# Flamingo-style two-layer block on one core: five maxima over partitions taken by TensorE and VectorE instead of GpSimd, and the order of every engine written out anew for each group

## The chip, the cores and the metric

The kernel runs on one core of a Trainium2 chip. The metric is the device time of one execution in microseconds, the median of several runs. The core has five engines that each work through their own instructions strictly in order: TensorE (PE in the profile; its weight loads are shown as PEld), VectorE (DVE), ScalarE (ACT), GpSimd (POOL) and SyncE (SP), which here only starts DMAs. They wait for one another by semaphores.

## The reference

Input x is 2 x 2048 tokens of 512 numbers, ctx is 2 x 128 tokens of 512. Four blocks follow one another; each adds tanh(gate) times its output to x, and each starts with a layer norm.

```python
x = x + tanh(g_xattn[0]) * attention(layernorm(x), ctx, Wq, Wkv, Wout)   # 8 heads, rotary q and k, 128 keys
x = x + tanh(g_ffn[0]) * ffn0(layernorm(x))      # ternary weights w_fc, w_proj with row scales,
                                                 # plus gate * low rank (u, fast_b, v); relu, square; 512-2048-512
x = x + tanh(g_xattn[1]) * (layernorm(x) @ W1.T + mean_over_ctx(ctx) @ W2.T + b)
x = x + tanh(g_ffn[1]) * ffn1(layernorm(x))      # int8-like activations, ternary weights w1, w2
                                                 # scaled by their mean |w|; exact gelu; 512-2048-512
```

Ternary weights are round(w / scale) clipped to -1, 0, 1; the scale of ffn0 is the mean |w| of a row, that of ffn1 the mean over the matrix. The weights arrive as float32 and are quantised inside the kernel.

## The kernel before, in words

**Tiling.** The 4096 tokens are cut into 16 groups of 256 (GROUPS; two tiles t of 128 tokens each). Every group g runs through the same steps: ln1, q projection (`q`), rotary, scores (`s`, four units n of one tile and half the heads), softmax (`max`, `exp`, `sum`, `norm`), attention times v (`pv`), output projection (`wo`), ln2, low-rank rows (`low`), first ffn (`up` in 8 units of two 128-row blocks, `down` in 8 pieces: 4 for each tile), ln3, the mix (`wx`), ln4, the second ffn (`w1` in 8 pieces, gelu, `w2`), and the store. Float32 activations enter matmuls as a pair of fp16 parts (hi and lo): ACT writes the hi part, DVE or POOL the rest, and a transposing DMA (from SP) turns them.

**Setting up.** Ahead of and among group 0 stand the steps that prepare the weights (`prepare` on each engine). Three of the weights (Wq, Wout, the mix's W1) and k, v and the low-rank v are scaled by their largest |value| before they are split into fp16 pairs. Each such maximum is taken in two steps: DVE reduces along the free dimension into one column (`abs_max`, into wmax or kvmax), and POOL's `partition_all_reduce` (L701, in `largest`) takes the largest of the 128 partitions and writes it to all of them (wmaxa, kvmaxa). There are five calls: Wq; k and v together; Wout and v of the low rank together; a bound on the hidden values (bmax to bmaxa, from which the scale rho of the hidden layer comes); and W1 of the mix. `weight_scale`, `kv_scale` and `hidden_scale` on DVE wait for them. The eight pieces of w_fc and w_proj are compared with thresholds on DVE (`signs`, L1052 and L1058), turned by PE (`tern`, L1481) and copied by ACT (`evac`, L807). The first `up` of group 0 needs all of w_fc, the row scales (`row_scale`, L1532 on PE and L1240 on DVE) and the low-rank rows of group 0.

**What sets the order.** No scheduler decides it. A table gives every step of every engine a place, a number; `moments` sorts the numbers of an engine, and `run` issues the steps whose number has come (`due` for the groups' steps, `here` for preparation). In the kernel before, table AT has one number per step, and group g uses it with g x 65536 added; groups 0, 1, 2, 14 and 15 have numbers of their own in table OWN. So groups 3 to 13 follow one another in one fixed pattern. On PE that pattern is, from one low-rank product to the next (g is the group in the first ffn, g+1 is in its attention, g-1 and g-2 are in the second ffn):

```text
low.g up0.g w2(t1).g-2 q0.g+1 q1.g+1 up1.g up2.g up3.g up4.g s0.g+1 wx1.g-1 up5.g s1 s2 up6.g s3 up7.g
w1(0..2).g-1 down0.g w1(3..5).g-1 down1.g down2.g down3.g w1(6).g-1 pv0 down4.g pv1 w1(7).g-1 wo0 wo1 w2(t0).g-1
down5.g down6.g down7.g wx0.g
```

**Places the prediction speaks of.** `low_rows` (L1609) writes the low-rank product to PSUM; ACT copies it as bf16 (`low_first`, L910); DVE makes the three-part bf16 tile tlow (`low_parts`, L1335 to L1340); the last matmul of each block of `up` (L1633) reads tlow, the first time in unit 0. `down` (L1645) waits for POOL's `hid_low` (L674), the lo part of the hidden values, two units for each piece. `out_proj` (`wo`, L1596) waits for the DVE lo part of the attention output (L1269). `scores` (L1570) waits for the four DMAs of `pair_heads` (q_in), which wait for the chain of rotary (DVE L1282 to L1285, POOL L669, ACT L875, DVE L1269) after `q_proj` (L1551).

## Time and profile before

| what | us |
|---|---|
| median of 3 runs | 1346.24 |
| lowest and highest of them | 1342.70, 1351.59 |
| span of the profiled execution, first to last instruction | 1340.0 |
| PE, DVE, ACT, POOL busy in it | 1135.0, 974.3, 788.0, 597.8 |

The profiled execution's own device time is not listed apart from the runs; its span lies 6.2 us under their median, and that much is taken as what lies around a span. Rows of the trace give start and length in microseconds of an instruction (or of a run of like ones, with xcount), then its engine, line, operation and tiles; a bracket at the end says how long the engine stood idle before it and whose result ended the wait. "issue" there means that the profile shows no wait: the engine was fetching or setting something up. Durations of pipelined matmuls overlap, so PE's work is better read from start to start.

### The profile page before, as it was taken

To read this page: it belongs to the slowest core of one execution; us is meant where nothing else is said; L and a number is where in the kernel's file an instruction comes from. 1 tells how busy PE (TensorE), PEld (TensorE's weight loads), DVE (VectorE), ACT (ScalarE), POOL (GpSimd) and SP (SyncE) were. 2 spreads that over 40 slices of the span, in tenths; PEclk is the share of its full clock that TensorE was granted. 3 is DMA by queue.
4 is the path that set the end of the run, shared out by engine and by line. 5 is a ranking of instruction groups with operands and counts; after the bars stand their busy time and mean duration, and the time that the engine had idled before them with its cause. 6 is when DMAs were issued, how large, how long until landed. Compare 5 with 4: busy or idle time off the path is not lost.

```text
span 1340.0 us, 19939 instructions
## 1 busy us (share of the span) xinstructions
PE 1135.0 (85%) x7092; PEld 695.2 (52%) x7380; DVE 974.3 (73%) x2017; ACT 788.0 (59%) x1509; POOL 597.8 (45%) x569
## 2 busy tenths in 40 slices
PE   4353777989898999999999999999999988899975
PEld 3332545546374646555564747464656556475621
DVE  3895587887758676877778686868687776877574
ACT  2455773839465574838384656657483838475523
POOL 1221254645534535455463555454545435363430
PEclk9666898999999999999999999999999999999997
DMA  6957744353423444443635343444444343524132
GB/s 220 298 179 214 238 135 97 78 111 71 91 67 84 98 87 100 87 97 81 130 79 100 70 87 77 96 98 87 99 87 87 87 99 74 114 55 86 24 67 51
DMA packets 302241, 140.28 MB, mean 105 GB/s; under 512 B 258096, under 2 KB 276016, under 8 KB 300464
## 3 DMA queue, kind: packets, MB, share of 16 engines
q1 hardware_dynamic: 299840, 136.62, 44.4%
q10 hardware_dynamic: 2304, 2.40, 0.6%
q8 instruction: 57, 0.93, 0.3%
q14 instruction: 40, 0.33, 0.1%
HBM read 57.97 MB, written 9.18 MB: 50 GB/s over the span
## 4 chain that ended last, share of the span: by engine, by line
DVE 27%; PE 27%; ACT 21%; POOL 12%; issue 9%; DMA 3%; SPq 1%; DVEq 0%; POOLq 0%; ACTq 0%
ACT e L882 6%; PE ps L1693 5%; PE ps L1645 5%; PE ps L1629 4%; DVE st L1256 4%; PE ps L1551 3%; PE ps L1596 3%; ACT rl L920 3%; POOL rs L649 2%; DVE amax L986 2%; ACT hid L925 2%; ACT sq L931 2%; POOL hid L674 2%; POOL e L679 2%; POOL r L692 2%
## 5 line engine op out<-in xcount | busy, mean ns | idle before, releaser
L1629 PE MATMUL ps<-xT,fcT 128*128 128x256 f16 x2048 | 261.1, 275 | 1.9 <-DVE scbc L1240 1.0
L1645 PE MATMUL ps<-pjT,hid 128*128 128x512 fp8e4 x1024 | 239.4, 385 | 24.1 <-POOL hid L674 22.0
L649 POOL TENSOR_TENSOR rs<-ve,nhalf 128x1 f32<-128x1 f32 x160 | 100.6, 629 | 289.1 <-DVE ve L1261 220.0
L1629 PEld LDWEIGHTS ps<-xT,fcT 128*128 128x128 fp8e4 x2048 | 201.0, 99 | 33.7 <-ACT rl L920 4.3
L674 POOL TENSOR_TENSOR hid<-sq,hid 128x512 f16<-128x512 f32 x128 | 163.0, 1280 | 101.8 <-ACT sq L931 101.8
L1645 PEld LDWEIGHTS ps<-pjT,hid 128*128 128x128 f16 x1024 | 98.5, 99 | 100.8 <-issue 4.9
L1693 PE MATMUL ps<-w2T,hT 128*128 128x512 fp8e4 x512 | 130.1, 413 | 12.5 <-DMA hT<-q 12.5
L1681 PE MATMUL ps<-w1T,q4T 128*128 128x512 fp8e4 x512 | 127.9, 390 | 15.0 <-DMA q4T<-x16b 6.5
L920 ACT ACTIVATE rl<-ps,rsf 128x256 f32<-128x256 f32 x256 | 106.6, 470 | 38.4 <-PE ps L1633 38.2
L679 POOL TENSOR_TENSOR e<-e,einv 128x512 f32<-128x512 f32 x64 | 73.1, 1142 | 125.7 <-DVE einv L1303 116.1
L882 ACT ACTIVATE e<-ps,nmb,sig 128x128 f32<-128x128 f32 x256 | 113.0, 455 | 13.3 <-DVE nmb L1299 13.0
L1269 DVE TENSOR_TENSOR qT<-e,qT 128x512 f16<-128x512 f32 x96 | 79.6, 830 | 50.9 <-ACT qT L893 28.6
L1551 PE MATMUL ps<-pt,wq 128*128 128x256 f16 x768 | 88.9, 276 | 13.2 <-DMA pt<-x16a 11.7
L1661 PE MATMUL ps<-wx,xT 128*128 128x512 f16 x384 | 92.2, 392 | 7.1 <-DMA xT<-x16b 7.1
L1402 DVE SCALAR_TENSOR_TENSOR h<-ps,dqs,b1bc 128x512 f32<-128x512 f32 x128 | 91.6, 740 | 8.8 <-PE ps L1681 8.3
L1633 PE MATMUL ps<-tlow,lowA 128*128 128x256 bf16 x256 | 71.2, 278 | 30.1 <-DVE tlow L1340 30.1
L1596 PE MATMUL ps<-wo,qS 128*128 128x512 f16 x384 | 86.3, 381 | 9.1 <-DVE qS L1269 9.1
L952 ACT ACTIVATE q<-h 128x2048 f16<-128x2048 f32 x32 | 61.1, 1908 | 52.4 <-DVE h L1413 52.4
L1551 PEld LDWEIGHTS ps<-pt,wq 128*128 128x128 f16 x768 | 75.9, 99 | 26.5 <-issue 14.7
L1693 PEld LDWEIGHTS ps<-w2T,hT 128*128 128x128 f16 x512 | 53.2, 105 | 64.6 <-issue 18.7
L669 POOL TENSOR_TENSOR e<-e 128x512 f32<-128x512 f32 x32 | 43.9, 1371 | 92.5 <-DVE e L1285 84.5
L875 ACT ACTIVATE qT<-e 128x512 f16<-128x512 f32 x32 | 20.1, 627 | 109.1 <-POOL e L669 109.1
(202 smaller groups left out, 2112.1 us busy)
## 6 DMA issues: line engine op xcount, KB each, us to landing
qS<-qT SPq DMA_DIRECT2D x128, 64.0 KB, 2.1
xb<-in_x SPq DMA_DIRECT2D x16, 512.0 KB, 4.8
out<-r SPq DMA_DIRECT2D x32, 256.0 KB, 2.6
xa<-in_x SPq DMA_DIRECT2D x15, 512.0 KB, 4.0
rope<-in_rope SPq DMA_DIRECT2D x16, 384.0 KB, 3.6
h<-in_w1T SPq DMA_DIRECT2D x6, 1024.0 KB, 6.5
h<-in_w2T SPq DMA_DIRECT2D x6, 1024.0 KB, 7.3
h<-in_wkvT SPq DMA_DIRECT2D x2, 1024.0 KB, 15.3
```

What stands on the lines that cost most here:

```text
L649: pool.tensor_tensor(rs[:, n, t:t + 1], ve[:, n, t:t + 1], nhalf[:, :], ALU.pow).then_inc(done, 1)
L674: pool.tensor_tensor(flat[:, 1, :], sq[:, m % 2, :], flat[:, 0, :], ALU.subtract).then_inc(hid_lo, 1)
L679: pool.tensor_tensor(view, view, einv[:, n, :].unsqueeze(2).broadcast_to([P, 4, S]), ALU.mult)\
L882: last = act.activation(e[:, n, a * S:(a + 1) * S], att_bank(2 + n)[:, a * S:(a + 1) * S], ACT.Exp, bias=nmb[:, n, a:a + 1], scale=sig[:, ...
L920: act.activation(rl[:, m % 2, a * G:(a + 1) * G], ps[:, FFN0 + m % 2, a * G:(a + 1) * G], ACT.Relu, scale=rsf[:, 2 * m + a:2 * m + a + 1]) ...
L1551: mm = pe.matmul(att_bank(hg)[:, a * G:(a + 1) * G], wq[:, ws, k, c:c + P], xT1[:, xs, k, :], start=(n == 0 and k == 0), stop=(n == 2 and ...
L1596: mm = pe.matmul(att_bank(8 + t), ao[:, xs, k, t * P:(t + 1) * P], wo[:, ws, k, :], start=(n == 0 and k == 0), stop=(n == 2 and k == KC - 1))
L1629: pe.matmul(dst, fcT[:, k, f * P:(f + 1) * P], xT2[:, xs, k, :], start=(xs == 0 and k == 0), stop=False)
L1645: mm = pe.matmul(ps[:, FFN0 + t, :], hid[:, xs, c, t * P:(t + 1) * P], pjT[:, c, :], start=(c == 0 and xs == 0), stop=(c == FC - 1 and xs ...
L1661: mm = pe.matmul(back_bank(t), xT3[:, xs, k, t * P:(t + 1) * P], wx[:, ws, k, :], start=(n == 0 and k == 0), stop=(n == 2 and k == KC - 1))
L1681: mm = pe.matmul(back_bank(2 + u), q4T[:, k, t * P:(t + 1) * P], w1T[:, k, n * 512:(n + 1) * 512], start=(k == 0), stop=(k == KC - 1))
L1693: mm = pe.matmul(back_bank(10 + t), hT[:, t, c, :], w2T[:, c, :], start=(c == 0), stop=(c == FC - 1))
```

## The change

Two things are changed.

1. `partition_all_reduce` and POOL's five calls are gone. For each of the five maxima DVE now multiplies the identity by the column (`spread_diag`: a 128x128 diagonal, one or two of them in the new tile dg), PE multiplies a matrix of ones by it (`spread`: every partition then holds the whole column along its free dimension, in PSUM), and DVE takes the maximum along that row (`largest`). The matmul is float32. Five pieces of PSUM are used for it (SPREAD), in banks of the attention and of the second ffn; the first scores wait for the third maximum, the mean's matmul for the fifth.
2. The tables AT and OWN, with numbers in nanoseconds that repeat from group 3 to 13, are replaced by one table ORDER that gives each step of each group a rank on its engine. Every group has its own row of it. PREP holds ranks in the same numbering.

```diff
+        SPREAD = ((ATT0 + 2, 1), (ATT0 + 2, 2), (ATT0 + 2, 2), (BACK0 + 2, 1), (BACK0 + 2, 1))
...
-        AT = dict(
-            PE=dict(up=(195289, 200771, 211516, 211832, 213196, 215372, 223295, 232242),
...
+        ORDER = dict(
+            PE=dict(
+                up=((35, 36, 37, 39, 40, 41, 44, 46), (64, 65, 66, 70, 74, 75, 79, 80),
...
-            def largest(ready, count, done, dst, src):
-
-                pool.wait_ge(ready, count)
-                pool.partition_all_reduce(dst, src, P, RMAXOP).then_inc(done, 1)
...
+            def spread_diag(n, ready, count, cols):
+
+                dve.wait_ge(ready, count)
+                if n == 0:
+                    dve.wait_ge(c_const, 5)
+                else:
+                    dve.wait_ge(c_mxps, n)
+                for j, col in enumerate(cols):
+                    last = dve.tensor_scalar(dg[:, j, :], ident[:, :], col, None, ALU.mult)
+                last.then_inc(c_mxd, 1)
+
+            def largest(n, dst):
+
+                dve.wait_ge(c_mxps, n + 1)
+                dve.tensor_reduce(dst, spread_to(n).rearrange("p (c n) -> p c n", n=P), axis=AX.X, op=ALU.max)\
+                    .then_inc(c_mx, 1)
+                dve.wait_ge(c_mx, n + 1)
...
-                dve.wait_ge(c_wmaxa, n + 1)
+                largest(n, wmaxa[:, a:b])
...
-                dve.wait_ge(c_bndmax, 1)
+                largest(3, bmaxa[:, :])
...
+            def spread(n):
+
+                if n > 0:
+                    pe.wait_ge(c_mx, n)
+                pe.wait_ge(c_mxd, n + 1)
+                pe.matmul(spread_to(n), ones[:, :], dg[:, 0:SPREAD[n][1], :].rearrange("p c n -> p (c n)"),
+                          start=True, stop=True).then_inc(c_mxps, 1)
...
-                    pe.wait_ge(c_low, 3)
+                    pe.wait_ge(c_mx, 5)
...
                 if first(g) and n == 0:
+                    pe.wait_ge(c_mx, 3)
                     pe.wait_ge(c_kblk, 1)
```

How POOL's instructions stand at the start of the program. Before, from the first rsqrt of ln1 of group 0 (L649) to the last softmax `norm` of group 0 (L679); L701 is the all-reduce, and each row that says only ISA is an instruction of the kind that sets the engine up for the operation behind it:

```order
L649 TENSOR_TENSOR rs<-ve,nhalf 128x1
L701 ISA
L701 ISA wmaxa<-wmax 128x1
L649 ISA
L649 TENSOR_TENSOR rs<-ve,nhalf 128x1
...
L679 TENSOR_TENSOR e<-e,einv 128x512
L701 ISA
L701 ISA bmaxa<-bmax 128x1
L679 ISA
L679 TENSOR_TENSOR e<-e,einv 128x512
L701 ISA
L701 ISA wmaxa<-wmax 128x1
```

Now, the same place (L719 rsqrt, L723 the lo part of x, L786 the context sums, L766 rotary of k, L791 a clearing of lowF, L739 rotary of q, L749 `norm`):

```order
L719 TENSOR_TENSOR rs<-ve,nhalf 128x1 x2
L723 TENSOR_TENSOR x16a<-xa,x16a 128x512
L786 TENSOR_TENSOR r<-ones,csum 128x128 x8
L723 TENSOR_TENSOR x16a<-xa,x16a 128x512
L766 TENSOR_TENSOR x3n<-x3n,rl 128x512 x2
L791 MEMSET x3n 128x2048
L739 TENSOR_TENSOR e<-e 128x512 x2
L719 TENSOR_TENSOR rs<-ve,nhalf 128x1 x2
L723 TENSOR_TENSOR x16a<-xa,x16a 128x512 x2
L749 TENSOR_TENSOR e<-e,einv 128x512 x4
```

No set-up instruction is left between them, the four norms follow one another, and ln1 of group 1 (rsqrt and lo part) has moved ahead of them.

PE's instructions in the steady part, around the low-rank product of group 8 (L1609 before). L1629 and L1633 are a block of `up`, L1691 and L1693 are `w2`, L1551 is `q`, L1661 `wx`, L1645 `down`:

```order
L1645 MATMUL ps<-pjT,hid 128x512 x8
L1661 MATMUL ps<-wx,xT 128x512 x12
L1609 MATMUL ps<-xT,vrep 128x256 x12
L1629 MATMUL ps<-xT,fcT 128x256 x8
L1633 MATMUL ps<-tlow,lowA 128x256
L1629 MATMUL ps<-xT,fcT 128x256 x8
L1633 MATMUL ps<-tlow,lowA 128x256
L1691 LDWEIGHTS hT
L1693 MATMUL ps<-w2T,hT 128x512 x16
L1551 MATMUL ps<-pt,wq 128x256 x48
```

Now, the same place (L1698 the low-rank product, L1718 and L1722 `up`, L1780 and L1782 `w2`, L1750 `wx`, L1639 `q`, L1659 scores):

```order
L1782 MATMUL ps<-w2T,hT 128x512 x16
L1750 MATMUL ps<-wx,xT 128x512 x12
L1639 MATMUL ps<-pt,wq 128x256 x24
L1698 MATMUL ps<-xT,vrep 128x256 x12
L1639 MATMUL ps<-pt,wq 128x256 x24
L1780 LDWEIGHTS hT
L1782 MATMUL ps<-w2T,hT 128x512 x16
L1718 MATMUL ps<-xT,fcT 128x256 x8
L1722 MATMUL ps<-tlow,lowA 128x256
...
L1659 MATMUL ps<-kv,qS 128x256 x6
```

Before, `up` stood directly behind the low-rank product; now half of `q` and a `w2` stand between. The next group is written otherwise again: behind its low-rank product comes only the `w2`, and then the first scores. In groups 3 to 12 something stands there each time (`w2`, `wx`, or both, at times with half of `q`), in group 13 nothing.

PE again, later in the same group: from the last piece of `w1` (L1681) that stood before `down1`, over `pv` (L1584), to `wo` (L1596). Before:

```order
L1645 MATMUL ps<-pjT,hid 128x512 x8
L1642 LDWEIGHTS hid
L1645 MATMUL ps<-pjT,hid 128x512 x8
L1679 LDWEIGHTS q4T
L1681 MATMUL ps<-w1T,q4T 128x512 x4
L1584 MATMUL ps<-pt,kv 64x256 x12
L1642 LDWEIGHTS hid
L1645 MATMUL ps<-pjT,hid 128x512 x8
L1584 MATMUL ps<-pt,kv 64x256 x12
L1679 LDWEIGHTS q4T
L1681 MATMUL ps<-w1T,q4T 128x512 x4
L1596 MATMUL ps<-wo,qS 128x512 x24
```

Now (L1734 `down`, L1770 `w1`, L1673 `pv`, L1685 `wo`):

```order
L1734 MATMUL ps<-pjT,hid 128x512 x8
L1673 MATMUL ps<-pt,kv 64x256 x12
L1731 LDWEIGHTS hid
L1734 MATMUL ps<-pjT,hid 128x512 x8
L1673 MATMUL ps<-pt,kv 64x256 x12
L1731 LDWEIGHTS hid
L1734 MATMUL ps<-pjT,hid 128x512 x8
L1768 LDWEIGHTS q4T
L1770 MATMUL ps<-w1T,q4T 128x512 x4
L1685 MATMUL ps<-wo,qS 128x512 x24
```

Both `pv` stand earlier among the `down` pieces, `down4` (first piece of the second tile) has moved ahead of `down1`, and `down3`, which needs the last hidden values, now stands behind the second `pv`.

## Rows read from the trace of the kernel before

**Rows 1.** The page's head and its first part: busy time and share of each engine

```profile
span 1340.0 us, 19939 instructions
PE 1135.0 (85%) x7092; PEld 695.2 (52%) x7380; DVE 974.3 (73%) x2017; ACT 788.0 (59%) x1509; POOL 597.8 (45%) x569
```

**Rows 2.** Two stretches: length; busy PE, PEld, DVE, ACT, POOL; PE clock; DMA share; GB/s

```profile
0.00:153.40 153.40, 67.59 (x377) 46.29 (x378) 99.87 (x205) 75.84 (x128) 31.73 (x43) 0.73 0.72 226
...
480.00:1056.00 576.00, 536.68 (x3413) 329.16 (x3553) 431.04 (x922) 356.08 (x705) 288.07 (x272) 0.97 0.44 89
```

**Rows 3.** PE's waits from 480 to 1056 us: total, times, longest

```profile
PE ps L1633 <- DVE tlow L1340: 18.6, 8, 2.3
PE ps L1645 <- POOL hid L674: 15.6, 8, 1.9
PE ps L1596 <- DVE qS L1269: 4.0, 8, 0.5
```

**Rows 4.** PE in order of time, one group of the fixed pattern

```profile
655.28 1.47 PE L1609 MATMUL ps<-xT,vrep 128*128 128x256 f16 x12
...
659.94 0.39 PE L1633 MATMUL ps<-tlow,lowA 128*128 128x256 bf16 x1 [2.31 <-DVE tlow L1340]
660.12 1.92 PE L1629 MATMUL ps<-xT,fcT 128*128 128x256 f16 x8
...
662.04 4.29 PE L1693 MATMUL ps<-w2T,hT 128*128 128x512 fp8e4 x16
666.17 5.40 PE L1551 MATMUL ps<-pt,wq 128*128 128x256 f16 x48
671.41 1.04 PE L1629 MATMUL ps<-xT,fcT 128*128 128x256 f16 x8
...
679.51 0.82 PE L1570 MATMUL ps<-kv,qS 128*128 128x256 f16 x6
...
703.37 2.67 PE L1645 MATMUL ps<-pjT,hid 128*128 128x512 fp8e4 x8 [1.95 <-POOL hid L674]
...
717.87 3.62 PE L1693 MATMUL ps<-w2T,hT 128*128 128x512 fp8e4 x16
```

**Rows 5.** POOL in order of time, 15 to 120 us

```profile
18.33 0.38 POOL L701 PARTITION_ALL_REDUCE wmaxa<-wmax  x1 [8.16 <-issue]
26.04 0.59 POOL L649 TENSOR_TENSOR rs<-ve,nhalf 128x1 f32<-128x1 f32 x1 [7.33 <-issue]
...
88.52 2.43 POOL L701 PARTITION_ALL_REDUCE bmaxa<-bmax  x1 [5.89 <-issue]
99.87 2.04 POOL L679 TENSOR_TENSOR e<-e,einv 128x512 f32<-128x512 f32 x1 [8.91 <-DVE einv L1303]
108.83 0.79 POOL L701 PARTITION_ALL_REDUCE wmaxa<-wmax  x1 [6.92 <-issue]
119.20 1.03 POOL L679 TENSOR_TENSOR e<-e,einv 128x512 f32<-128x512 f32 x1 [9.58 <-issue]
```

**Rows 6.** DVE in order of time, 10 to 147 us

```profile
10.53 2.29 DVE L986 TENSOR_REDUCE wmax<-hid 128x1 f32<-128x2048 f32 x1 [1.00 <-DMA hid<-in_wqT]
...
26.66 1.38 DVE L1265 TENSOR_SCALAR xa<-xa,mv,rs 128x512 f32<-128x512 f32 x1 [7.57 <-POOL rs L649]
...
103.98 0.17 DVE L1303 RECIPROCAL einv<-esum 128x4 f32<-128x4 f32 x1
...
120.98 0.69 DVE L1269 TENSOR_TENSOR qT<-e,qT 128x512 f16<-128x512 f32 x1 [9.61 <-ACT qT L893]
...
130.03 0.87 DVE L1234 TENSOR_SCALAR r<-ident,scd 128x128 f32<-128x128 f32 x4
...
146.67 0.17 DVE L1245 TENSOR_REDUCE wmean<-ps 128x2 f32<-128x8 f32 x1 [3.24 <-PE ps L1537]
```

**Rows 7.** PE in order of time, the two float32 matmuls by the matrix of ones

```profile
131.04 2.05 PE L1532 MATMUL ps<-r,ones 128*128 128x512 f32 x2 [3.08 <-DVE r L1234]
...
146.04 0.60 PE L1537 MATMUL ps<-wsum,ones 128*128 128x8 f32 x2 [6.20 <-ACT hT L857]
```

More of the change, by code:

```diff
@@ new lines, in build @@
+        PREP = dict(
+            PE=dict(k=(1, 2), v=(3, 4), low=(7,), mix=(11,), tern=(5, 18, 19, 20, 21, 23, 25, 26), low_t=(22,),
+                    row_scale=(28,), mean=(32,), spread=(0, 6, 8, 12, 16)),
+            DVE=dict(const=(0,), ctx_sum=(7,), rot_k=(9, 11), wq_max=(1,), wq_scale=(5,), k_max=(12,), wq_lo=(8,),
+                     v_max=(15,), kv_scale=(18,), k_lo=(20,), v_lo=(21, 22), signs=(14, 17, 25, 50, 54, 57, 60, 64),
+                     thr=(13, 16, 24, 32, 34, 42, 44, 63), wo_max=(10,), v_top=(19,), wo_scale=(23,), k_other=(37,),
+                     wo_lo=(31,), mix_row=(59,), low_rank=(33,), v_parts=(62,), wx_max=(38,), hidden=(40,),
+                     wx_scale=(48,), wx_lo=(67,), row_scale=(69,), mean=(76,), k_now=(36,), diag=(66,),
+                     round=(77, 79, 84, 87, 93, 95, 100, 114), clip=(80, 81, 88, 91, 96, 108, 109, 120)),
+            ACT=dict(wq=(1,), k_hi=(6,), v_hi=(7, 8), tanh=(5,), wo=(10,), kv_save=(17,),
+                     evac=(22, 25, 29, 33, 36, 38, 41, 44), rows=(3, 4, 9, 12, 14, 15, 16, 18), low=(37,), wx=(32,),
+                     sums=(30, 35, 39, 42, 45, 46, 47, 49), lift=(51, 52, 56, 58, 62, 75, 76, 82)),
+            POOL=dict(rot_k=(5, 6), csb=(3,), low_zero=(7,), above=(0, 0, 0, 0, 0, 0, 0, 0)),
+            SP=dict(ctx=(1,), wk=(2,), wq=(0,), wv=(3,),
+                    piece=(5, 7, 11, 15, 16, 17, 19, 21, 26, 28, 31, 34, 36, 30, 33, 39, 40, 41, 45, 46, 49, 50, 52, 57),
+                    wo=(4,), wc=(6,), wx=(8,), b1=(18,), k_pair=(20,)))
@@ L449, in moments @@
+        placed = {}
+        for eng, tables in ORDER.items():
+            for name, rows in tables.items():
+                for g, places in enumerate(rows):
+                    for k, p in enumerate(places):
+                        placed.setdefault((eng, name, p), []).append((k, g))
         def moments(eng):
@@ L716, in prepare @@
                     rotate_k(hg)
-                for _ in here("POOL", "wq_max", p):
-                    largest(c_wmax, 1, c_wmaxa, wmaxa[:, 0:1], wmax[:, 0:1])
-                for _ in here("POOL", "kv_max", p):
-                    largest(c_kvmax, 2, c_kvmaxa, kvmaxa[:, :], kvmax[:, :])
                 for _ in here("POOL", "csb", p):
@@ L727, in prepare @@
                     last.then_inc(c_csb, 1)
-                for _ in here("POOL", "wo_max", p):
-                    largest(c_wmax, 3, c_wmaxa, wmaxa[:, 1:3], wmax[:, 1:3])
                 for _ in here("POOL", "low_zero", p):
@@ L735, in prepare @@
                         signs_above(q)
-                for _ in here("POOL", "bound", p):
-                    largest(c_bnd, 4, c_bndmax, bmaxa[:, :], bmax[:, :])
-                for _ in here("POOL", "wx_max", p):
-                    largest(c_wmax, 4, c_wmaxa, wmaxa[:, 3:4], wmax[:, 3:4])
             def run():
@@ L1171, in prepare @@
                     abs_max(kvmax[:, 1:2], ps[:, 0:2, :].rearrange("p b n -> p (b n)"), c_kvmax)
+                    spread_diag(1, c_kvmax, 2, [kvmax[:, 0:1], kvmax[:, 1:2]])
                 for _ in here("DVE", "kv_scale", p):
[L1173 removed]
+                    largest(1, kvmaxa[:, :])
                     dve.tensor_scalar(kvmaxa[:, :], kvmaxa[:, :], TINY, 1.0 / TOP, ALU.max, ALU.mult).then_inc(c_kvinv, 1)
@@ L1483, in ternary @@
                     mm.then_inc(c_tern, 1)
+            def spread(n):
[4 more added lines that the diff above has]
+                          start=True, stop=True).then_inc(c_mxps, 1)
             def prepare(p):
+                for n in here("PE", "spread", p):
+                    spread(n)
                 for hg in here("PE", "k", p):
```

334 lines of the change are left out of this document (158 added, 176 removed), and 66 rows, old and new, of tables (down, exp, h, hid).

## The prediction

> **What bounds the kernel now.** I read the page first, then the busy time by stretches, then PE's waits in the steady part, then the engines in order of time in one steady group and at the start.
>
> The page [rows 1] shows PE busy 1135.0 of 1340.0 us, DVE 974.3 and nothing else near. So the kernel is a TensorE kernel with 205 us in which PE stands still. The reader is to see where those lie [rows 2]. In the first 153.4 us, until `up` of group 0 begins, PE is busy 67.6 and DVE 99.9: PE loses 86 us there. From 480 to 1056 us, eight groups of the fixed pattern (each wait of rows 3 comes eight times), it is busy 536.7 of 576, so a group takes 72.0 us with 67.1 busy and 4.9 idle.
>
> PE's waits in the eight groups [rows 3] are three and recur each time: 2.3 us in `up` for tlow, 1.95 for the hidden values in `down`, 0.5 before `wo`; together 38.2 of the 39.3 us. One group in order of time [rows 4] shows them and something behind them. After the 2.31 us for tlow, eight matmuls of `up` take 1.92 us, and 1.04 elsewhere; `w2` takes 4.29, and 3.62 at 717.87. That is PE at the lower of its two clock levels (1.2 in place of 2.4 GHz) for a few us. The mean granted clock of the stretch is 0.97 [rows 2]: 6% of 72 us, 4.3 us, at half speed, which costs 2.2 us per group. So PE's own work at full clock is 72.0 - 4.9 - 2.2 = 64.9 us, and 7.1 us per group could be had.
>
> At the start the bound is a chain over several engines. POOL [rows 5] does little, but around every all-reduce it has long gaps that are "issue": 5.9 to 6.9 us ahead of it (8.16 for the first, which counts some waiting for data), 7.3 to 9.6 us behind it before the next ordinary instruction. The all-reduce itself shows 0.4 to 2.4 us. So one such call takes POOL out for about 15 us.
>
> Here a rule of the Trainium skill speaks against the change. "GPSIMD Engine Reference", section 4, gives GpSimd as the only option for a reduction across partitions, and its table in 4.1 says not to use VectorE for one. This trace does not bear it out as a price: the reduction is short, the change of code around it long, and the same page's glossary says that libraries of this engine are loaded at run time, with which the gaps agree.
>
> **The change, part by part.**
>
> Removed: five calls on POOL. Three of them hold up something. The first: the reduction on DVE ends at 12.8 us, POOL's result is there at 18.7, and the second rsqrt of ln1 runs only at 26.04; DVE waits 7.57 us for that [rows 5, 6]. The fourth: between 88.5 and 99.9 the third `norm` waits. The fifth: POOL leaves `norm` at 101.9, does the maximum at 108.83, and starts the last `norm` at 119.20, though its input einv was ready at 104.15 [rows 5, 6]. ACT, DVE (9.61 us idle at 120.98) and PE all stand behind it: 15.0 us of the chain that ends in `wo`, ln2 and `up`.
>
> Added: per maximum one or two products of the identity, a float32 matmul of 128 or 256 columns, one reduction from PSUM. From rows: the four products at L1234 take 0.87 us, so 0.22 each [rows 6]. The matmul with 512 columns takes 2.05 us and the one with 8 takes 0.60 [rows 7]: for 128 or 256 columns 0.6 to 1.0. No row shows a reduction of 128 or 256 numbers from PSUM; between the one of 8 numbers (0.17) and the 0.87 of four products, 512 numbers, lies what I take, 0.4. Round trip: 0.3 + 0.8 + 0.4, 1.5 us against 5.9 for the first call. DVE's own time for five: seven products, 1.5, and five reductions, 2.0, so 3.5 us more on an engine that is busy 99.9 of 153.4. PE: 4 us where it is mostly idle, so nothing. The new waits: PE has `low`, `q` and the mix queued behind `spread`, and DVE has all its queue behind `largest`. The order has other work between a product and its reduction in all five cases but for the first, so I price the waits at 0 to 5 us, 1 taken.
>
> What is late next at the start: DVE. It is idle 53.5 of 153.4 us [rows 2], of which some 9 lie ahead of the first weight's maximum at 10.53 [rows 6]. If all its gaps went but those, the start would be 44 us shorter, less 3.5. If only the 9.6 at 120.98 went, less 3.5, it would be 6. I take the 9.6, the 7.6 at 26.66, 2 of the 5.9 of the first call and some 5 of the later small ones that hang on the same chain (`wo`, ln2), less 3.5 and 1: 20 us. DMA is a second bound: its engines are busy 0.72 of 153.4 us [rows 2], 110 us, so it does not forbid 133. Bounds 5 and 40, value 20.
>
> Moved: everything. For the steady part I look only at what PE waits for.
> - tlow: from the end of the low-rank product (1.3 us from start to start) to the L1633 at 659.94 is 3.3 us, of which `up` hides 0.9 [rows 4]. In groups 3 to 12 now `w2`, `wx` or both lie between. All 2.3 us go; in group 13 they stay. Ten groups. (Sixteen matmuls of 512 columns take 3.62 [rows 4], 0.22 each with the overlap taken off: so `w2` 3.5, `wx` 2.6, a piece of `down` 1.75, of `w1` 0.87.)
> - hidden values: `down3` stood about 10.4 us of PE work behind `up7`, and 1.95 us too early. Now it stands 8.6 to 12.9 us behind it, in half of the groups far enough. But in the groups where it is nearer, `up7` itself stands behind more `w1`. I take half, 1.0; bounds 0 and 1.95.
> - `wo`: one to six pieces more between `pv` and it; 0.5 goes.
> - the lower clock followed each long wait. If 4 of 5 us of waits go, most of its 2.2 goes: 1.4 taken, 0 to 2.2.
> - new waits, unseen in this trace: scores now stand early. Before, from the end of `q0` (about 668.9) to the first scores at 679.51 are 10.6 us, in which rotary, heads and four DMAs fit [rows 4]. Now in group 8 11.4 us of PE work lie between, in group 9 about 9.1. So up to 1.5 us can come in some groups, and like amounts elsewhere; I take 1.0, bounds 0 and 7 (below).
> Sum: 2.3 + 1.0 + 0.5 + 1.4 - 1.0 = 4.2 us per group, 42 us for ten. Bounds 0 and 7.1 per group.
> Groups 0 to 2 and 13 to 15 had an order of their own already; the last 90 us are the latencies of the last group. 0 taken, -15 to +15.
>
> Total: 1340.0 - 20 - 42 = 1278 us span, and with the 6.2 us around it 1284 against the median of 1346.24.
>
> **The rivals.**
> - Only the start gains, as each wait of PE that goes in the steady part comes back at another place (DVE is 75% busy there and ACT 62% [rows 2], and every engine is in order). For it: the old pattern was laid out for a period of 65.5 us and took 72.0, so a written order promises more than it gives. Against: the three waits are each hidden in a way that can be counted. 1326.
> - Only the steady part gains: DVE and the arriving weights bound the start. For it: DVE is by far the busiest engine up to 153.4 us [rows 2], and each of its 44 us of gaps could move rather than go. Against: 9.6 us of idle right behind POOL's gap. 1304.
> - Both gain little, and what POOL gives back at the start is used up by the new order: 1340.
> - The maxima cost DVE more than they free. Its 3.5 us of new work and up to 5 of waits lengthen a start that it bounds, by 8.5 us, and the order gives nothing: 1355. That is what the Trainium skill's rule above would lead to. Against: the 15.0 us of POOL on the chain.
> - Slower: the scores. On POOL the rotary of group g+1 (L669) now stands behind the x3 lo part and add_cb of the second tile of group g-1, which hang on the chain `down`, ln3. If these come late, the rotary does, and PE, which has all of `up` queued behind the first scores, stands. It decides from where this wait exceeds what is gained, 62 us over 11 groups, 5.6 us each. At 8 us each, the time is 1284 + 88 = 1372. Against: POOL is busy only half of the time there, 288.1 of 576 us [rows 2].
>
> **How the numbers follow.** My forecast 0.60; only the start 0.15; only the steady part 0.12; both little 0.05; the costly maxima 0.03; slower by the scores 0.05. A measurement of this kernel tells about 1%, 13.5 us, from no change. The first three are faster by more: 0.87; the next two are within it, 0.08; the last is slower, 0.05. The forecast's own range is 1262 to 1308. To 8 in 10 it goes up to include the two half-cases: 1255 to 1327. The lower end is 30 us for the start and 6 us per group.
>
> **What would show it right or wrong.** In the profile after: no "issue" gaps above 3 us on POOL in the first 150 us; `up` of group 0 starting near 133 instead of 153.4; the first maximum ready near 15 us; PE's wait for tlow below 5 us in all of 480 to 1056 instead of 18.6; groups of 68 us instead of 72.0, and a clock of 0.98 or more. Wrong: a new PE wait for `q` heads (scores) of more than 3 us per group, `up` of group 0 starting after 148, or a group of 71 us or more.

## The result, and the profile after

| | median, us | lowest to highest | runs |
|---|---|---|---|
| before | 1344.47 | 1341.48 to 1351.59 | 4 |
| after | 1253.58 | 1252.10 to 1255.48 | 4 |

The ratio is 0.9316, 95% interval 0.9284 to 0.9349: 91 us less, where 62 were forecast; the time lies 1.4 us below the range. The profiled execution took 1254.16 us for a span of 1252.1.

The page's head and first part, after:

```profile
span 1252.1 us, 19955 instructions
PE 1120.1 (89%) x7102; PEld 697.7 (56%) x7390; DVE 975.9 (78%) x2029; ACT 783.7 (63%) x1509; POOL 577.6 (46%) x564
```

Against [rows 1] DVE's work is up by 1.6 us and PE's down by 15, with more instructions; what fell is PE's standing still, from 205 us to 132.

The span is best cut at the low-rank products, one to a group. Their starts are 148.69 (group 0), 362.63 (3), 1087.81 (13) before, and 129.35, 327.55, 1005.95 after. The first three of the four stretches of each kernel (columns as in [rows 2]), before:

```profile
0.00:148.69 148.69, 63.91 (x349) 43.49 (x350) 96.04 (x201) 71.88 (x125) 31.73 (x43) 0.73 0.73 231
148.69:362.63 213.94, 184.28 (x1208) 115.08 (x1252) 169.06 (x314) 137.00 (x265) 103.79 (x93) 0.97 0.44 106
362.63:1087.81 725.18, 673.92 (x4280) 412.96 (x4461) 542.19 (x1154) 449.02 (x890) 361.70 (x339) 0.97 0.44 91
```

and after:

```profile
0.00:129.35 129.35, 77.22 (x423) 53.85 (x424) 106.17 (x229) 78.46 (x130) 33.02 (x41) 0.78 0.91 277
129.35:327.55 198.20, 178.27 (x1144) 111.00 (x1188) 155.61 (x299) 130.49 (x262) 101.06 (x93) 0.96 0.50 111
327.55:1005.95 678.40, 655.09 (x4281) 409.54 (x4460) 547.03 (x1156) 443.58 (x888) 349.14 (x339) 1.00 0.47 97
```

| stretch | before | after | gain | forecast |
|---|---|---|---|---|
| start, to the low rank of group 0 | 148.7 | 129.4 | 19.3 | 20 |
| groups 0 to 2 | 213.9 | 198.2 | 15.7 | 0 |
| groups 3 to 12 | 725.2 | 678.4 | 46.8 | 42 |
| groups 13 to 15 | 252.2 | 246.1 | 6.1 | 0 |

Around the span lie 2.1 us, where the forecast put 6.2. Single traces differ by a few us: over all runs below, groups 0 to 2 take 213.9 to 217.2 us with the old order throughout (nine traces, the kernel before the shortest) and 196.7 to 201.0 with the new one (seven).

In the ten steady groups PE's work is the same (4280 and 4281 matmuls). Its busy time fell by 18.8 us as the clock went from 0.97 to 1.00, its idle time from 51.3 to 23.3. At the start 74 more matmuls (q of group 1 and the last `tern` piece among them) are done in 19.3 us less, and DVE is busy for 106 of 129 us; the DMA engines for 0.91 of it.

PE's waits in the ten groups, after (total, times, longest), beside [rows 3]:

```profile
PE ps L1639 <- issue: 5.5, 6, 2.0
PE ps L1673 <- DMA pt<-qT: 4.8, 7, 2.1
PE ps L1698 <- issue: 3.5, 5, 1.0
PE ps L1659 <- DMA qS<-qT: 2.2, 3, 0.8
```

None of the three old waits is in the list. What is left is spread over many places, none in each group: `q` for its input (L1639), `pv` for its transposes (L1673), the low-rank product (L1698), the scores (L1659). "Issue" was explained ahead of the rows as fetching or setting something up; on PE it is not that here: the product of group 8, at 670.38 us, starts 0.1 us after the transpose of its input has landed (670.28). PE in order of time at the place of [rows 4]:

```profile
670.38 1.47 PE L1698 MATMUL ps<-xT,vrep 128*128 128x256 f16 x12 [1.03 <-issue]
671.68 2.78 PE L1639 MATMUL ps<-pt,wq 128*128 128x256 f16 x24
674.30 3.62 PE L1782 MATMUL ps<-w2T,hT 128*128 128x512 fp8e4 x16
677.76 1.04 PE L1718 MATMUL ps<-xT,fcT 128*128 128x256 f16 x8
678.63 0.27 PE L1722 MATMUL ps<-tlow,lowA 128*128 128x256 bf16 x1
```

`w2` takes 3.62 where it took 4.29 behind the wait, and `up`'s eight matmuls 1.04 instead of 1.92.

POOL at the start, all of its `norm` instructions of group 0, where [rows 5] had the last two at 99.87 and 119.20 behind gaps of 8.9 and 9.6 us:

```profile
76.33 1.04 POOL L749 TENSOR_TENSOR e<-e,einv 128x512 f32<-128x512 f32 x1 [2.28 <-DVE einv L1381]
82.50 2.04 POOL L749 TENSOR_TENSOR e<-e,einv 128x512 f32<-128x512 f32 x2 [5.13 <-DVE einv L1381]
89.51 1.99 POOL L749 TENSOR_TENSOR e<-e,einv 128x512 f32<-128x512 f32 x1 [4.97 <-DVE einv L1381]
```

Each of the three rows begins when its own input (einv) has come, and the last ends at 91.5. The first maximum on DVE, product and reduction, with PE's matmul between them (PE L1568):

```profile
10.90 0.29 DVE L1065 TENSOR_SCALAR dg<-ident,wmax 128x128 f32<-128x128 f32 x1
...
13.57 0.29 DVE L1071 TENSOR_REDUCE wmaxa<-ps 128x1 f32<-128x128 f32 x1
```

```profile
11.24 0.80 PE L1568 MATMUL ps<-dg,ones 128*128 128x128 f32 x2 [11.24 <-DVE dg L1065]
37.02 1.19 PE L1568 MATMUL ps<-dg,ones 128*128 128x256 f32 x2 [0.46 <-DVE dg L1065]
```

From 10.90 to the end of the matmul, 12.04, plus the 0.29 of the reduction is 1.4 us of latency (1.5 forecast). DVE had ln1 between, so the maximum was there at 13.86 (near 15 forecast).

### The profile page after: what moved, and what is told of

It is laid out like the page before. It is cut to its first block, busy times and chain, and to the rows that moved or that the text cites. A ratio compares the mean times of both kernels' runs of the same rounds, so it can differ in the third digit from the quotient of the medians.

```text
span 1252.1 us, 19955 instructions
## 1 busy us (share of the span) xinstructions
PE 1120.1 (89%) x7102; PEld 697.7 (56%) x7390; DVE 975.9 (78%) x2029; ACT 783.7 (63%) x1509; POOL 577.6 (46%) x564
## 4 chain that ended last, share of the span: by engine, by line
PE 30%; DVE 27%; ACT 20%; DMA 11%; issue 6%; POOL 4%; SPq 2%; POOLq 0%; ACTq 0%; DVEq 0%
PE ps L1734 8%; ACT e L937 5%; PE ps L1782 4%; PE ps L1685 4%; PE ps L1718 3%; ACT rl L975 3%; PE ps L1770 3%; DVE st L1334 3%; DMA pt<-qT 3%; PE ps L1750 3%; ACT hid L980 2%; DVE qT L1347 2%; ACT sq L986 2%; DVE amax L1041 2%; DMA hT<-q 2%
## 5 line engine op out<-in xcount | busy, mean ns | idle before, releaser
L1718 PE MATMUL ps<-xT,fcT 128*128 128x256 f16 x2048 | 261.4, 276 | 7.1 <-ACT rl L975 7.1
L719 POOL TENSOR_TENSOR rs<-ve,nhalf 128x1 f32<-128x1 f32 x160 | 105.3, 660 | 321.7 <-DVE ve L1339 226.4
L1734 PE MATMUL ps<-pjT,hid 128*128 128x512 fp8e4 x1024 | 232.6, 380 | 2.6 <-issue 1.3
L1718 PEld LDWEIGHTS ps<-xT,fcT 128*128 128x128 fp8e4 x2048 | 202.2, 99 | 42.2 <-ACT rl L975 10.2
L744 POOL TENSOR_TENSOR hid<-sq,hid 128x512 f16<-128x512 f32 x128 | 155.9, 1221 | 114.0 <-ACT sq L986 113.6
L1734 PEld LDWEIGHTS ps<-pjT,hid 128*128 128x128 f16 x1024 | 97.7, 98 | 98.9 <-issue 1.3
L1782 PE MATMUL ps<-w2T,hT 128*128 128x512 fp8e4 x512 | 119.9, 389 | 23.0 <-DMA hT<-q 22.8
L1770 PE MATMUL ps<-w1T,q4T 128*128 128x512 fp8e4 x512 | 122.9, 383 | 5.6 <-DMA q4T<-x16b 4.5
L1347 DVE TENSOR_TENSOR qT<-e,qT 128x512 f16<-128x512 f32 x96 | 88.9, 935 | 25.0 <-ACT qT L948 16.1
L749 POOL TENSOR_TENSOR e<-e,einv 128x512 f32<-128x512 f32 x64 | 68.9, 1081 | 67.9 <-DVE einv L1381 67.8
L1750 PE MATMUL ps<-wx,xT 128*128 128x512 f16 x384 | 89.5, 383 | 10.7 <-DMA xT<-x16b 10.6
L1041 DVE TENSOR_REDUCE amax<-h 128x1 f32<-128x2048 f32 x32 | 73.0, 2281 | 31.6 <-ACT h L996 31.6
L1639 PE MATMUL ps<-pt,wq 128*128 128x256 f16 x768 | 89.2, 276 | 8.1 <-issue 6.6
L1639 PEld LDWEIGHTS ps<-pt,wq 128*128 128x128 f16 x768 | 75.6, 99 | 22.6 <-issue 12.3
L1685 PE MATMUL ps<-wo,qS 128*128 128x512 f16 x384 | 85.5, 379 | 0.0
L980 ACT ACTIVATE hid<-rl 128x512 f16<-128x512 f32 x128 | 80.6, 630 | 5.0
L1782 PEld LDWEIGHTS ps<-w2T,hT 128*128 128x128 f16 x512 | 50.2, 100 | 57.3 <-issue 5.5
L986 ACT ACTIVATE sq<-rl 128x512 f32<-128x512 f32 x128 | 78.5, 613 | 0.0
```

What stands on the lines that cost most here:

```text
L744: pool.tensor_tensor(flat[:, 1, :], sq[:, m % 2, :], flat[:, 0, :], ALU.subtract).then_inc(hid_lo, 1)
L980: act.activation(hid[:, 0, 2 * m:2 * m + 2, :].rearrange("p c n -> p (c n)"), rl[:, m % 2, :], ACT.Square)\
L1347: dve.tensor_tensor(dst, src, hi, ALU.subtract).then_inc(done, 1)
L1639: mm = pe.matmul(att_bank(hg)[:, a * G:(a + 1) * G], wq[:, ws, k, c:c + P], xT1[:, xs, k, :], start=(n == 0 and k == 0), stop=(n == 2 and ...
L1685: mm = pe.matmul(att_bank(8 + t), ao[:, xs, k, t * P:(t + 1) * P], wo[:, ws, k, :], start=(n == 0 and k == 0), stop=(n == 2 and k == KC - 1))
L1718: pe.matmul(dst, fcT[:, k, f * P:(f + 1) * P], xT2[:, xs, k, :], start=(xs == 0 and k == 0), stop=False)
```

## Which half of the change does it

The edits of the orders are given below as they read on an engine; all steps that are not named stay where they were.

**The maxima alone.** The order of before, with the new maxima.

```diff
 DVE, POOL, PE: order of the kernel before
-POOL partition_all_reduce x5
+DVE spread_diag / PE spread / DVE largest x5, at the place of the old calls
+DVE maximum of the low-rank v behind kv_scale, that of the mix's W1 behind low_rank
```

> The kernel before with the new maxima and its old order (two steps had to be moved on VectorE, the maximum of the low-rank v behind kv_scale and that of the mix's weight behind low_rank, since the diagonals are made in turn). Theory A, the start was held by GpSimd's gaps: the last norm comes near 104 instead of 119 us, VectorE's 9.6 us idle goes, up of group 0 starts 6 to 12 us earlier: 1332 to 1338 against 1344. Theory B, the gaps were covered and only the new order gains: 1342 to 1348.

Measured 1333.81 (ratio 0.9898, 0.984 to 0.9955). The low-rank product of group 0 starts at 135.99, 12.7 us earlier; groups 3 to 12 have the old period (725.5 us for the ten) and the three old waits. DVE is busy for 978.1 us in all, 3.8 more than before.

**The order alone.** The new order, with five calls on POOL put between its steps, in three places.

```diff
 DVE, POOL, PE: order of the kernel after
-DVE spread_diag / PE spread / DVE largest x5
+POOL partition_all_reduce: Wq; k and v, then Wout; bound, then W1
```

> The kernel after with its order, but the maxima on GpSimd again (put as early as their inputs allow, in four visits instead of five). Theory A: the start gets 10 to 20 us longer than in the kernel after, the rest stays: 1264 to 1274. Theory B: 1253 to 1258. If the new order of the steady groups were good only behind the new start, more than 1280.

Measured 1264.58 (0.9389, 0.9325 to 0.9453), 11 us above after; the product of group 0 starts at 141.43, 12.1 later. POOL in order of time:

```profile
21.27 0.38 POOL L827 PARTITION_ALL_REDUCE wmaxa<-wmax  x1 [7.55 <-issue]
29.18 1.15 POOL L779 TENSOR_TENSOR x16a<-xa,x16a 128x512 f16<-128x512 f32 x1 [7.53 <-issue]
...
76.08 0.46 POOL L827 PARTITION_ALL_REDUCE bmaxa<-bmax  x1 [5.88 <-issue]
79.33 0.56 POOL L827 PARTITION_ALL_REDUCE wmaxa<-wmax  x1 [2.78 <-DVE wmax L1112]
87.96 2.71 POOL L779 TENSOR_TENSOR x16a<-xa,x16a 128x512 f16<-128x512 f32 x2 [8.07 <-issue]
```

The change of kind costs 5.9 to 7.6 us into the all-reduce and 7.5 to 8.1 out of it, by these rows; two calls in a row pay it once (the second waits 2.78 us for its data, not for "issue"). The maxima are worth 12.7 us in the old order and 11 to 12 in the new one, so of the start's 19.3 some 12 are theirs and 7 the order's.

**By stretches.** The new start and the order of before from the low-rank product of group 3, 0 and 13 on, and the reverse.

```diff
 all engines
-order after
+order after up to low.g3 (1), low.g0 (2), low.g13 (3); from there order before
+order and maxima before up to low.g3; from there order after (4)
```

> New maxima and new order up to the low-rank product of group 3, the old order from there. If start and steady part gain apart from one another, the traces say 19 us for the start and 16 for groups 0 to 2: 1307 to 1312. If the gain of the start is given back later when the old pattern follows: 1325 or more.

> GpSimd's maxima and old order up to the low-rank product of group 3, the new order from there. If the parts are independent: 47 us for the ten steady groups and 6 at the end, 1289 to 1294, and this gain and that of the kernel with the new start add up to 91. If the steady gain needs the new start: 1305 or more.

> New maxima and new order up to the low-rank product of group 0, the old order from there on. Theory A (the gain of 15.7 us in groups 0 to 2 is the new order's own, and about 6 us of it is work of group 1 and of the ternary pieces taken ahead of the product): 1322 to 1328, so 13 to 16 us more than the kernel that has the new order up to group 3 (1311.1), and the product of group 0 at 129 to 131 us. Rival B (groups 0 to 2 gain because the start left the other engines ahead, whichever order follows): 1308 to 1316, as the one up to group 3.

> The new kernel up to the low-rank product of group 13, the old order from there to the end. Theory A (the last three groups' own order is worth the 6.1 us that the traces differ by): 1258 to 1262, the product of group 13 at 1006. Rival B (the end is shorter only because it is entered with the engines further ahead, which stays): 1254 or less. Rival C (the two orders don't fit at the seam, as at group 3 where it cost some 8 us): 1264 or more.

| kernel | us | ratio to before | low of g0, g3, g13 |
|---|---|---|---|
| (1) new up to g3 | 1311.10 | 0.9724 (0.9667 to 0.9781) | 127.98, 328.40, 1052.06 |
| (2) new up to g0 | 1322.63 | 0.9835 (0.9785 to 0.9885) | 129.69, 342.40, 1071.08 |
| (3) new up to g13 | 1262.02 | 0.9378 (0.9347 to 0.9409) | 129.40, 330.42, 1009.04 |
| (4) new from g3 on | 1302.52 | 0.9654 (0.9596 to 0.9711) | 150.93, 367.73, 1055.36 |

(1) and (4) gain 37 and 46 us (against 1348.1 in their series); the whole gained 91, and of the 8 us between them the seam of (4) has most: its first group, 3, takes 79.8 us, where it takes 72.0 in the kernel after. From group 0 to 3 (2) takes 212.7 us and (1) 200.4: 12.3 us belong to the new order of groups 0 to 2, and 1 to 4 come from work moved into the start (the old order behind the old start takes 213.9 to 216.9). The medians of the two, 11.5 us apart, say the same, with less sharpness than they seem to have: the four times of (2) lie between 1315.75 and 1329.25, and the traced one is the longest, while that of (1) is its shortest. (The expectation had 13 to 16.) (3) needs 253.2 us from group 13 to the end, after 246.1: the 6 to 7 us of the end are its own order's too.

## What a wait of PE is worth: four moves in the kernel before

The forecast took each wait for something that a filler (a step put into the place of the wait) removes. Tried alone, on PE only:

```diff
 PE, before, groups 3 to 13
-low.g up0.g w2(t1).g-2 q0.g+1 q1.g+1
+low.g w2(t1).g-2 up0.g q0.g+1 q1.g+1      (M1: w2 fills)
+low.g q0.g+1 up0.g w2(t1).g-2 q1.g+1      (M2: half of q fills)
 PE, before, groups 4 to 13
-down2.g down3.g w1(6).g-1 pv0 down4.g
+down2.g down4.g w1(6).g-1 pv0 down3.g     (M3: hidden values later)
```

> The kernel before with one step moved: on PE the w2 that stood behind up0 now stands between the low-rank product and up0, in groups 3 to 13. Theory A: the tlow wait of 2.3 us a group goes, and about 1 us of lower clock with it; 25 to 36 us for eleven groups, 1310 to 1320 (of 1346). Rival B: the old order is bound by a chain through other engines with the period of 72 us, and the wait goes to another place (down3 or q): less than 8 us, above 1338.

> The kernel before with one pair of steps exchanged: on PE down4 (first piece of the second tile) stands where down3 stood and down3 where down4 stood, in groups 4 to 13. Theory A: the 1.95 us wait for the hidden values goes, with up to 1.5 of lower clock; 15 to 30 us, 1316 to 1331. Rival B: it comes back at another place: less than 8 us, above 1338. The fourth piece of the first tile ends later, so ln3 of that tile starts some 7 us later, which A takes to be hidden.

> The kernel before with both moves of PE's steps (w2 ahead of up0; down4 and down3 exchanged), the old maxima. Theory A (the waits are independent): the sum of the two gains, 40 to 60 us, 1286 to 1306, the clock 0.99 to 1.00 in the steady part, so that two moves on one engine give what the whole new table gives there (46.8 us). Rival B: the sum falls short by half or more, above 1315, since the table's changes on the other engines are needed.

> The kernel before with one step moved on PE: the first half of q of the next group, 2.6 us, stands between the low-rank product and up0 instead of behind up0 and w2 (groups 3 to 13). The move of w2 to this place had the tlow wait gone and gained only 15 us, since w2 then waited 2.1 us for its own input. Theory A (a wait goes for good if the step that fills it has its input ready and gains slack itself): 1.9 to 3.3 us a group, 1310 to 1328, without a new wait of over 0.5 us a group. Rival B (the old order is so tight that whatever fills the place, the wait returns): 1335 or more.

| kernel | us | ratio to before | period, us |
|---|---|---|---|
| M1 | 1335.01 | 0.9882 (0.9842 to 0.9921) | 71.0 to 72.8 |
| M3 | 1343.71 | 0.9953 (0.9931 to 0.9974) | 70.0 to 72.5 |
| M1 and M3 | 1335.46 | 0.9892 (0.985 to 0.9935) | 71.0 to 73.1 |
| M2 | 1398.68 | 1.04 (1.0373 to 1.0428) | 75 to 79 |

All four miss what theory A expected, and the wait's return (rival B) is nearer each time. The waits of PE from 480 to 1056 us in M1 and M3 together say why:

```profile
PE ps L1818 <- DMA hT<-q: 16.6, 8, 2.1
PE ps L1709 <- DMA pt<-qT: 10.8, 16, 1.0
PE ps L1721 <- DVE qS L1394: 8.9, 8, 1.2
PE ps L1754 <- ACT rl L1045: 6.4, 8, 0.8
```

```profile
480.00:1056.00 576.00, 532.61 (x3440) 329.45 (x3583) 438.12 (x926) 363.08 (x714) 293.03 (x274) 0.99 0.45 91
```

tlow and the hidden values are gone from the list, and in their place `w2`, now ahead of `up0`, waits 2.1 for its own input (L1818), `pv`, moved up by a piece of `down`, waits 1.35 for its (L1709, in two parts), `wo` (L1721) 1.1 instead of 0.5, and `up` (L1754) 0.8. PE's idle time is 5.3 us a group, where it was 4.9. The 1.2 us that most groups gained are clock alone: busy time 65.7 instead of 67.1, at 0.99. Here the shorter waits cost less of it.

M2 is the same thing at a high price: 53 us slower, which rival B's "1335 or more" covers in words only. PE in order of time:

```profile
675.56 1.47 PE L1734 MATMUL ps<-xT,vrep 128*128 128x256 f16 x12
682.47 5.28 PE L1676 MATMUL ps<-pt,wq 128*128 128x256 f16 x24 [5.44 <-issue]
687.55 1.27 PE L1754 MATMUL ps<-xT,fcT 128*128 128x256 f16 x8
```

`q` needs ln1 of the second tile, turned by a DMA that in this order lands only at 682.38 us: the wait shows as "issue", 5.44 us, and the 24 matmuls behind it take 5.28 us at the lower clock where they take 2.78. The expectation took q's input for ready, and that was wrong.

**Moving the producers too.** M2 once more in groups 4 to 12, with ln1 of the second tile moved up on the other four engines, and in a second step the scale of gelu behind ln2 and ln1:

```diff
 DVE  -x1#1 q5_sc#1.g-2 ln2#1 q5#1.g-2 x4#0 ln1_st#1.g+1 x2#1 ln1#1.g+1
      +x1#1 ln1_st#1.g+1 q5_sc#1.g-2 ln2#1 ln1#1.g+1 q5#1.g-2 x4#0 x2#1     (M4)
      +x1#1 ln1_st#1.g+1 ln2#1 ln1#1.g+1 q5_sc#1.g-2 q5#1.g-2 x4#0 x2#1     (M5)
 ACT  hi part of it ahead of the rounding of gelu
 POOL its rsqrt and lo part moved up (M5: the rsqrt of gelu behind the lo part of ln2)
 SP   both its transposes ahead of that of gelu
```

> The kernel before with the same step of PE moved as in the run that was 53 us slower (first half of q between the low-rank product and up0; here groups 4 to 12), and with it what makes its input: on VectorE the second tile's ln1 ahead of the scale of gelu and ahead of its rounding, on ScalarE and GpSimd its fp16 parts, and the two transposes of it on SyncE's queue ahead of that of the gelu. Theory A (a wait of PE goes only if the other engines' orders move with PE's): the tlow wait goes and q0 does not wait; 2 to 3.3 us for nine groups, 1313 to 1330. Rival B (the other engines have no place for it; what is late then is the gelu's own transpose or the hidden values): 1335 or more. If q0 still waits 5 us for its input, 1380 or more.

> The last kernel but two (first half of q between the low-rank product and up0, ln1 moved with it), which had the tlow wait replaced by 2.2 us of q0 for its input and made no difference, with one more companion: on VectorE the 3 us of scale of gelu (amax) now stand behind ln2 and ln1 of the second tile instead of ahead of them, and GpSimd's rsqrt of it behind the lo part of ln2. Theory A (it was that which held up both inputs): q0 waits less than 0.5 us, the low-rank product too comes earlier; 2.5 to 4 us in nine groups, 1310 to 1325. Rival B (the wait moves on once more, to w2 for its gelu or to the hidden values): 1335 or more.

M4: 1344.09, ratio 0.9994 (0.9971 to 1.0017). M5: 1341.97, 0.9989 (0.9967 to 1.0011). So what M2 lacked are the producers, but they give no more than was lost: from group 4 to 13, where both have the move, M2 takes 695.1 us, M4 647.9 and the kernel before 648.8. (The other 7 of the 55 us between M2 and M4 lie outside these nine groups; M4 leaves groups 3 and 13 as they were.) PE's waits from 480 to 1056 us in M5:

```profile
PE ps L1771 <- POOL hid L800: 15.6, 8, 1.9
PE ps L1677 <- issue: 12.0, 8, 1.5
PE ps L1735 <- DVE r L1473: 6.1, 8, 0.8
PE ps L1755 <- ACT rl L1046: 5.7, 8, 0.7
PE ps L1722 <- DVE qS L1395: 4.0, 8, 0.5
```

The tlow wait of 2.3 us has become three of 1.5 (`q`, L1677), 0.8 (the low-rank product, L1735) and 0.7 (`up`, L1755). The hidden values (L1771) and `wo` (L1722) wait as before. The period is 71.2: idle time has grown from 4.9 to 5.5 us a group, but the granted clock of this stretch is 1.00. Rival B of both expectations held.

## What the steady part is made of: three moves in the kernel after

```diff
 PE, after, groups 3 to 12 (as an example, group 8)
-low.g q1.g+1 w2(t1).g-2 up0.g
+q1.g+1 w2(t1).g-2 low.g up0.g             (M6: product moved back)
+low.g up0.g q1.g+1 w2(t1).g-2             (M7: up0 moved forward)
 PE, after, those of groups 7 to 12 where down4 stands early (as an example, group 7)
-down0 down4 pv0 down1 pv1 down2 down3 ... down5
+down0 down1 pv0 down2 pv1 down3 down4 ... down5   (M8)
```

> The new kernel with one thing undone: in groups 3 to 12 the low-rank product stands again directly ahead of up0 on PE, all other steps in the new order. Theory A (each wait of PE in the steady part has its own price: idle 2.3 us a group for tlow, and about 1 more from the lower clock behind it): 2.3 to 3.5 us a group, 23 to 35 for ten, so 1277 to 1289 where the new kernel takes 1253.6; PE's wait for tlow about 20 us or more in the ten groups, the clock near 0.98. Rival B (the new order as a whole keeps the other engines ahead, and one wait more is made up elsewhere, as other waits shrink): less than 10 us more, below 1264.

> The new kernel with up0 moved forward on PE to stand directly behind the low-rank product in groups 3 to 12; in the run before the product was moved back to up0, and it cost 50 us where the wait itself is 2.3 a group. Theory H (the excess came from ScalarE and VectorE, which have the copy and the split of the product ahead of the rotary and the heads in their queues and so stood behind a product that came 4 to 7 us later): here the product stays where it is, so only the bare wait and its clock return, 23 to 35 us, 1277 to 1289. Rival B (the work between the product and up0 is worth 5 us a group whatever stands behind it): 1298 or more. Rival C (the wait is made up elsewhere): below 1264.

> The new kernel with the pieces of down of each of groups 3 to 12 put back in rising order in the same eight places on PE (where down4 stood ahead of down1 or down2 they change; in groups 3 to 6 and 9 nothing changes, so five or six groups are touched). Theory A (the wait for the last hidden values comes back where down3 stands 1.75 us nearer): 1 to 2 us in each touched group, 5 to 12 us, 1258 to 1266. Rival B (down3 has room there now, the exchange was free): within 3 us of 1253.6.

M6: 1303.43, ratio 0.9653 (0.9614 to 0.9693). M7: 1294.32, 0.9653 (0.958 to 0.9725). M8: 1253.50, 0.9331 (0.9291 to 0.9371). To leave nothing between the product and `up0` costs 40 to 50 us, nearly all that the new order gains in the steady part. PE's waits from 480 to 1056 us, first M6, then M7 (L1723 scores, L1786 `up` for tlow, L1846 `w2`):

```profile
PE ps L1723 <- DMA qS<-qT: 18.6, 10, 3.6
PE ps L1786 <- DVE tlow L1482: 9.1, 8, 1.1
PE ps L1846 <- DMA hT<-q: 8.0, 5, 2.2
```

```profile
PE ps L1786 <- DVE tlow L1482: 23.7, 8, 4.1
PE ps L1723 <- DMA qS<-qT: 5.7, 3, 2.4
```

In M6 the product comes later, and the bare tlow wait is only 1.1; but ACT and DVE have its copy and split in their queues ahead of rotary and heads and stand behind it (ACT waits 75.9 us for L1762 there, 24.4 after), so the scores wait for the heads. In M7 the product stays, and the ten groups take 71.8 us each, 3.9 more than after: 3.1 of idle and 0.8 of clock. 2.7 of the idle is the tlow wait itself: in most groups ACT and DVE come to the copy and the split later than in the kernel before, so that tlow is ready 2.0 to 4.9 us behind the product (3.1 in the kernel before). M6's groups take 72.3. M7 lies between what theory H and rival B expected: the place itself is worth about 4 us a group, and what the queues behind the product add in M6 is 0.5 by the two traces and nothing by the ratios, which are equal; M7's four times spread over 18 us. So that part is not shown. The order of the pieces of `down`, which the forecast gave half of 1.95 us, is worth nothing measurable here (the interval leaves room for some 5 us in all).

**Why the hidden values no longer wait.** The forecast looked for this in PE's own work between `up7` and `down3`. It is not there. That work was 10.4 us in groups 4 to 12 and is 6.9 to 12.8 in groups 3 to 12 now, less than 10.4 in seven of the ten, and 6.8 to 11.9 in M8; none of them waits for POOL. What has changed is how late the values are. From the end of `up7` to the end of the last `hid_low` POOL needs 12.5 us in groups 4 to 11 before (and in M3 and M5 too, which leave POOL's place for it and the scores as they were), and 4.0 to 7.5 in groups 3 to 12 after. POOL in order of time, before (group 7; L679 `norm`, L674 `hid_low`; `up7` ends at 690.8):

```profile
699.55 1.04 POOL L679 TENSOR_TENSOR e<-e,einv 128x512 f32<-128x512 f32 x1 [0.75 <-DVE einv L1303]
700.55 2.72 POOL L674 TENSOR_TENSOR hid<-sq,hid 128x512 f16<-128x512 f32 x2
```

and after (group 8; L749 and L744; `up7` ends at 700.6):

```profile
701.93 2.04 POOL L749 TENSOR_TENSOR e<-e,einv 128x512 f32<-128x512 f32 x2 [1.36 <-DVE einv L1381]
703.93 2.28 POOL L744 TENSOR_TENSOR hid<-sq,hid 128x512 f16<-128x512 f32 x2
```

In both, the last two `hid_low` stand behind the `norm` of the next group's last scores, which waits for their softmax. In groups 4 to 12 PE used to end these scores 2.0 us ahead of the end of `up7`; now it ends them 9.6 to 17.8 us ahead of it. No run moves the scores alone, so this is read from the rows and not tested.

**Two more fills at the end.** In the kernel after, the low-rank products of groups 13 and 15 still stand directly ahead of `up0`.

```diff
 PE, after
-wx0.g12 low.g13 up0.g13
+low.g13 wx0.g12 up0.g13
-low.g15 up0.g15 up1.g15 up2.g15 w2(t1).g13
+low.g15 w2(t1).g13 up0.g15 up1.g15 up2.g15
```

> The new kernel with the two places filled where the product of the low rank still stands directly ahead of up0 on PE in the last groups: wx0 of group 12 behind the product of group 13, w2 of group 13 behind the product of group 15. Theory A: both waits for tlow (2.1 us at most each) go, 2 to 4 us, 1249.5 to 1251.5. Rival B: the end is set by the last group's own chain and nothing changes: 1252.5 to 1254.5.

Measured 1263.21 (1260.61 to 1263.66 in five runs), 9.6 us slower. The product of group 13, moved up by one step, waits 2.87 us for ln2; the waits of `w2` for its input grow from 19.8 to 26.4 us from group 13 on. Neither rival had this; it is the result of M1 and M2 over again, in an order that has no slack left there. So no kernel measured is faster than the kernel after; M8 is level with it.

## Why the prediction was right, and where it was wrong

- **The start: right.** 19.3 us at the low-rank product, 21.5 at `up` of group 0 (131.86 for 153.38), against 20. The gaps of POOL are gone, and their removal alone is worth 12.7. The rule weighed in the prediction (the Trainium skill, "GPSIMD Engine Reference", sections 4 and 4.1, GpSimd as the only option for a reduction across partitions) is not borne out here: the way through PE and DVE has 1.4 us of latency, where the first call had 5.9 and kept POOL out for about 15. The cost on DVE was right too: the seven products take 1.8 us together and the five reductions 1.7 (0.29 for 128 numbers, 0.42 for 256), 3.5 as forecast; that DVE's whole busy time rose by only 1.6 comes from its other work.
- **Steady groups, idle: right in sum, by luck: two errors cancel.** -2.8 us a group were forecast (2.3 + 1.0 + 0.5 - 1.0), -2.8 came (51.3 to 23.3 for ten). But all of the hidden-values wait went, 1.95, not half, and not for the reason given. The prediction put `down3` "8.6 to 12.9 us" behind `up7` and gave half for the groups where it is far enough; in groups 3 and 4 it stands 6.9 behind, and no group waits, as the values are ready 4.0 to 7.5 us after `up7` instead of 12.5. In all, what went is 4.75 a group and what is new 2.0, about twice the 1.0 taken (`q` 0.55, `pv` 0.48, low rank 0.35, scores 0.22 and smaller ones).
- **Steady groups, clock: mis-sized.** "1.4 taken, 0 to 2.2": 1.9 came, nearly all that could, as the granted clock is now 1.00. 5 us of the miss.
- **The step that failed: "Groups 0 to 2 and 13 to 15 had an order of their own already; ... 0 taken".** They gave 15.7 and 6.1 us, 22 of the 30 us missed. That they had numbers of their own said nothing about how good these were. The runs show it as the order's work: 12.3 us in groups 0 to 2 between two kernels with the same start, 7 us at the end between two kernels equal up to group 13. What in these orders does it was not taken apart. [Rows 2] would have shown that something was to be had there, had the stretch from group 0 to 3 been asked for: 30 us of idle PE in three groups, double the steady rate. The range allowed 15 us for this term; it came to 22, with the clock and the next term on the same side. This term, the clock and what lies around the span are why the time lies below the range.
- **"6.2 us around it": wrong.** In the runs here the device time lies 1.75 to 3.1 us above the span of the same execution, 1.75 to 1.86 in those of the kernel before; the 6.2 was the distance of one execution to the median of others. 4 us.
- **Rivals.** "Each wait of PE that goes comes back at another place" did not hold for the change, but it is what happened in every partial move (M1 to M5, and the two fills at the end), though M1 kept 9 to 15 us, by the clock. It was given 0.15 for the change. The scores did not become the bound: 2.2 us in ten groups.

**Why the whole order gains what its parts do not.** I counted PE's own work between the end of a step and the step that needs it (lengths at full clock from the rows), mean of groups 4 to 11:

```text
                                before   after
q1 -> first scores                7.8      7.9
first scores -> pv0              23.5     26.2
pv1 -> wo of the second tile      3.5      6.6
wo -> low rank                   11.4     15.6
low rank -> up0                   0        5.4
down3 -> wx0                     19.1     14.5
wx0 -> w1 (first)                30.9     26.7
```

The old order has four links of the attention short at the same time and much room between `down`, the mix and the second ffn. The new one takes from there and gives to all links from the scores to `up0` at once, about 15 us along the chain. M1, M2 and M3 each made room in one place by moving a step so near to its own input that it waited in turn. Length counted from an order is no time, and no run swapped this surplus alone, so this is an argument that fits the runs, not a thing that they prove. A test that keeps the new order on one engine and the old one on the others was not made. Open is also which of the moves on DVE, ACT and POOL the steady part needs.
